# The order of a kernel's first transfers, on two queues in place of one, and half of its constant products

## The chip, the cores and the metric

One Trainium2 chip, one NeuronCore of it. The metric is device time in microseconds of one launch; the median of three runs of the kernel before is 424.43 us (423.6 to 425.7). Engines: PE is TensorE (matmul), PEld its weight load, DVE VectorE, ACT ScalarE, POOL GpSimd; SP is SyncE, which here only issues DMAs.

## The reference

2048 rows of 128 numbers pass through a feed-forward block, an attention block and the same feed-forward block again:

```python
x = x + 0.5 * ffn(layernorm(x), ...)   # the change is in this first one
x = x + attn(layernorm(x), ...)
x = x + 0.5 * ffn(layernorm(x), ...)

def ffn(x):                            # L=128 rows, N=16, D=128
    y1 = ln(x + mha(x))
    return ln(y1 + moe(y1))
def moe(x):                            # 8 experts, FF=512, at most S/8 rows each
    gates = softmax(x @ wg); idx = argmax(gates)
    # row kept if its place among the rows of its expert is under the cap
    h = disp @ w1 + b1;  y = h @ w2 + b2
    return where(keep, gate * y, 0)
```

The batch that `mha` attends over has one row, so its softmax is 1 and it is the product with the value weights and the output weights. No activation stands between `w1` and `w2`, so the two are multiplied to one 128x128 matrix per expert, and the biases to one row per expert.

## The kernel before

The 2048 rows are four chunks (g = 0 to 3) of four tiles of 128 rows. Each engine runs its own list of instructions. In the first feed-forward block the order on each engine is written by hand in the strings of ORDER; a word is a step and a chunk (or, for D and E, an expert or a tile). The engines meet only through semaphores.

The steps that matter here, all in the first block:

- X (DVE, POOL): statistics of the input rows of a chunk, waiting for its x_in, and the rsqrt on POOL.
- A (PE, ACT): transposes of the chunk (L1105) and the copy out. W (PE, DVE): the product of value and output weights, which waits for all six transfers of mha_in (L1169, L1172, L1175), with short runs of constant products between.
- P (PE, DVE, POOL): the product with that matrix (L1089), the addition on DVE (L780), statistics, and on POOL the rsqrt (L501). M (ACT): the normalised rows. C (PE, ACT): their transposes.
- D (PE): for expert e, waits for its two weights (w_in), then eight matmuls for w1 x w2 (L1199) and eight for its bias row (L1206). In D0, ahead of L1206, PE waits for b1_ready to be 2.
- b (POOL, L583): the copy that raises b1_ready to 2. It waits for fold_in to be 48, so for all three of b1_t, b2_t and sel.
- L, R, K: logits, the pick of the expert, its coefficient (the picks are L806 and L808 on DVE). B on POOL (L509): the addition of a bias to the input rows. H: the end of the folding. E: the experts of a tile.

The orders around the change, and the wait in step b:

```python
"pe":   "A0 W0 A1 P0 P1 D0 C0 D1 D2 L0 A2 C1 P2 R0 A3 D3 P3 K0 D4 L1 D5 D6 D7 R1 H0 K1 ..."
"act":  "A0 A1 M0 M1 C0 L0 A2 C1 A3 D0 K0 ..."
"dve":  "10 X0 X1 W0 X2 P0 P1 X3 L0 R0 P2 K0 P3 L1 ..."
"pool": "X0 X1 X2 b0 P0 P1 X3 D0 B0 B1 B2 B3 P2 P3 ..."

pool.wait_ge(fold_in, 16 * FOLD)          # FOLD = 3
pool.tensor_copy(b1_diag, b1_t).then_inc(b1_ready, 1)
```

Beside its work PE multiplies a constant tile by itself (keep_busy, L1157): START_WORK times at the start, and by IDLE_WORK before some steps, 12 times before C0 of the first block. Results of these are not read.

All loads are issued by SP: chunk 0 of x, the six of mha_in, chunks 1 to 3, the four of route_in, the three of fold_in, the four of const_in, then w1 and w2 of experts 0 to 7 (16 transfers of 256 KB), then what attention needs. ACT issues none.

Of the kernel before, what the change touches and what calls it, by code (L numbers as in the profile page):

```python
# [14 lines left out]
P = 128  # L15
# [3 lines left out]
G = 4  # L19
GT = T // G  # L20
GW = GT * P
E = 8
FF = 512
FC = FF // P
# [117 lines left out]
)  # L142


START_WORK = 20
IDLE_WORK = {"C0": (12, 0), "O3": (0, 4), "A3": (0, 3), "C3": (0, 26), "L3": (0, 4), "R3": (0, 7),
             "K3": (0, 2), "B3": (0, 1)}

# [6 lines left out]
def build(nc, a, out):  # L155
    with ExitStack() as ctx:
        def sb(name, shape, dt=F32):
            return ctx.enter_context(nc.sbuf_tensor(name, shape, dt))

        def sem(name):  # L160
            return ctx.enter_context(nc.semaphore(name))
# [4 lines left out]
        ident = sb("ident", [P, P])  # L166
# [7 lines left out]
        centre = sb("centre", [P, D])  # L174
# [34 lines left out]
        def rows(k):  # L209
# [28 lines left out]
        w1T = fold[:, 0:4096].rearrange("p (e c d) -> p e c d", e=E, c=FC)  # L238
        w2 = fold[:, 4096:8192].rearrange("p (e c d) -> p e c d", e=E, c=FC)
# [8 lines left out]
        wv = fold[:, 13568:13696]  # L248
        woT = fold[:, 13696:13824]
        bv = fold[:, 13824:13825]  # L250
        bv_rep = fold[:, 13952:14080]
        ob_rep = fold[:, 14080:14208]
# [21 lines left out]
        w_in = [sem(f"w_in{e}") for e in range(E)]  # L274
        packed_in, row_in = ([sem(f"{n}{c}") for c in range(G)] for n in ("packed_in", "row_in"))
        wo_in = sem("wo_in")
        const_in, mha_in, route_in, fold_in, att_in, rope_in, template_in = (sem(n) for n in
            ("const_in", "mha_in", "route_in", "fold_in", "att_in", "rope_in", "template_in"))
# [36 lines left out]
        def cols(g):  # L315
            return slice(GW * g, GW * (g + 1))
# [8 lines left out]
        def group(g):  # L325
            return slice(GT * g, GT * (g + 1))
# [9 lines left out]
        def normed_groups(kind):  # L336


            return {ROWS: 0, LN2: G - 1}.get(kind, G)
# [24 lines left out]
        def _(sp):  # L364
            def load_x(g):
                sp.dma_start(x_tm[:, group(g), :],
                             a["x"][cols(g), :].rearrange("(t p) d -> p t d", p=P)).then_inc(x_in[g], 16)

            load_x(0)
            for dst, src in ((ident[:], a["ident"]), (centre[:], a["centre"]), (wv, a["wv"]), (woT, a["woT"]), (bv, a["bv"]),  # L370
                             (ob_rep, a["ob"].partition_broadcast(P))):
                sp.dma_start(dst, src).then_inc(mha_in, 16)
            for g in range(1, G):
                load_x(g)
            for dst, src in ((g1c[:], a["g1c"]), (wg[:], a["wg"]), (tri_bf[:], a["tri"].bitcast(BF16)),
                             (rank[:], a["rank"].partition_broadcast(P))):
                sp.dma_start(dst, src).then_inc(route_in, 16)
            sp.dma_start(b1_t, a["b1_t"]).then_inc(fold_in, 16)
            sp.dma_start(b2_t, a["b2_t"]).then_inc(fold_in, 16)
            sp.dma_start(sel[:], a["sel"]).then_inc(fold_in, 16)  # L380
            for dst, src in ((lnb[:], a["lnb"].partition_broadcast(P)), (tile_is[:], a["tile_is"]),
                             (head_of[:], a["head_of"].bitcast(BF16)), (swap[:], a["swap"])):
                sp.dma_start(dst, src).then_inc(const_in, 16)
            for e in range(E):
                sp.dma_start(w1T[:, e, :, :], a["w1T"][e].rearrange("(p c) d -> p c d", c=FC)).then_inc(w_in[e], 16)
                sp.dma_start(w2[:, e, :, :], a["w2"][e].rearrange("(p c) d -> p c d", c=FC)).then_inc(w_in[e], 16)
            for dst, src in ((wqo[:, 0, :], a["wq"]), (wdu[:, 0, :], a["w_downT"]),
                             (wdu[:, 1, :], a["wk_up"]), (wdu[:, 2, :], a["wv_up"])):
                sp.dma_start(dst, src).then_inc(att_in, 16)
# [28 lines left out]
            for g in range(G):  # L418
                if g == HELD:
                    sp.wait_ge(branched, 1)  # L420
                for side in (1, 0):
                    w = 2 * g + 1 - side
                    sp.wait_ge(low_piece, w + 1)
                    dst = piece_dram[side, g].rearrange("b d two p n -> (d two p) b n")
# [27 lines left out]
            with sp.If(beyond_safe > 0):  # L452
# [11 lines left out]
                with sp.Fori(0, NG) as g:  # L464
# [4 lines left out]
                    dst = shift_dram[bass.ds(g * GH, GH), :].rearrange("h (t p) -> (h t) p", p=P)  # L469
# [156 lines left out]

        @block.scalar
        def _(act):
            def normalise(kind, n, g, src, dst):
                act.wait_ge(ln_offset[kind], normed_groups(kind) * n + g + 1)  # L630
                for t in range(GT * g, GT * (g + 1)):
                    ins = nc.scalar.activation(dst[:, t, :], src[:, t, :], ACT.Identity,  # L632
                                               bias=offset[:, t:t + 1], scale=rstd[:, t:t + 1])
                ins.then_inc(normed[kind], 1)
# [9 lines left out]
            def feed_forward(n):  # L644
                for step, g in steps(n, "act"):
                    q, bank = G * n + g, CHAIN + g % 2
                    if step == "A":
                        copy_turned(ROWS, n, g, bank, xT)
                    elif step == "M":
                        normalise(LN1, n, g, y, y)  # L650
                    elif step == "C":
                        act.wait_ge(route_in, 16 * ROUTE)
# [12 lines left out]
                    elif step == "E":  # L665
# [9 lines left out]
                        ins.then_inc(high_ready, 1)  # L675
                    elif step == "V":
                        normalise(LN2, n, g, y, y)
                    elif step == "S":
                        if g >= 2:
# [400 lines left out]
        def _(pe):  # L1080
# [73 lines left out]
            def keep_busy(count, bank=3):  # L1154

                for _ in range(count):
                    pe.matmul(ps[:, bank, :], idle[:, 0:P], idle[:], start=True, stop=True)  # L1157
# [131 lines left out]
            pe.wait_ge(idle_ready, 1)  # L1289
            keep_busy(START_WORK)  # L1290
            feed_forward(0)
# [12 lines left out]
            def scores(n, run):  # L1304

                k, _, banks = UNITS[n]
                c, g = BLOCKS[k]
                if n == 0 or UNITS[n - 1][0] != k and g == 0:
                    pe.wait_ge(packed_in[c], 16 * packed_dmas(c))
                    pe.wait_ge(row_in[c], 16 * SHIFT_DMAS)  # L1310
                if n < SLOTS:
                    slot_free(n)
                else:
                    pe.wait_ge(run.exp_done, n - SLOTS + 1)
                for i in range(len(banks[0])):
                    for b in range(2):
                        h, j, q, w, col = banks[b][i]
                        rows = slice(HALF * b, HALF * b + (USED if j >= GT * c else MASK_ROW))
                        pair = (GH * g + h) // 2
                        ins = pe.matmul(ps[:, 2 * (n % SLOTS) + b, col:col + w], tile_of(rows, 1, pair, j),  # L1320
                                        packed[rows, c, 0, pair, q - GW * c:q - GW * c + w], start=True, stop=True,
                                        tile_position=(HALF * b, 0))
                ins.then_inc(run.score_mm, 1)
# [185 lines left out]
```

## Time and profile before

| what | us |
|---|---|
| median of three runs | 424.43 |
| the profiled execution | 424.33 |
| its span | 422.5 |
| PE busy | 388.2 (92%) |
| ACT busy | 326.2 (77%) |
| DVE busy | 193.7 (46%) |
| POOL busy | 129.3 (31%) |

The span is the profiled execution from its first to its last recorded instruction; 1.8 us lie around it. Busy shares are of the whole span; a stage has its own. All times of rows below are counted from the start of the span. "Matmul busy" includes the constant products.

### The profile page before, as it was taken

Reading aid. Unit: us, or ns where it says so; the run is one execution under the profiler, and the core shown is the slowest. Engines: PE = TensorE matmul, PEld = TensorE weight load, DVE = VectorE, ACT = ScalarE, POOL = GpSimd, SP = SyncE. Lnnn points to the kernel's source line nnn. Section 1 sums busy time; section 2 is a strip of 40 time slices with the busy share of each in tenths; the row PEclk is TensorE's granted clock in tenths of the full one; section 3 lists DMA queues with packets and bytes.
Section 4 is the critical chain, followed back from the end, with each engine's and each line's share of the span. In section 5 each row is a group of like instructions: output and inputs, shape, how many; then the busy total and the mean of one; then the engine's idle time right before and its main releaser. Section 6 shows DMA issues by size and latency. Waiting matters only on the chain.

```text
span 422.5 us, 7542 instructions
## 1 busy us (share of the span) xinstructions
PE 388.2 (92%) x2708; PEld 130.5 (31%) x2711; DVE 193.7 (46%) x729; ACT 326.2 (77%) x466; POOL 129.3 (31%) x203
## 2 busy tenths in 40 slices
PE   7889999689979699999999999999999999999991
PEld 3577443234422132222222222222222222114530
DVE  4865698899844223314242232261332322303846
ACT  1245458386699689999999999999999999995131
POOL 1472788663210022100302210063122420110673
PEclk9999999999989799999999999999999999999996
DMA  5891900001993299600000000001000000000000
GB/s 143 294 347 26 116 2 2 0 1 63 237 256 52 87 217 252 98 2 2 0 2 2 0 2 2 0 2 28 0 2 0 2 27 0 2 2 0 1 26 25
DMA packets 17756, 24.52 MB, mean 58 GB/s; under 512 B 2616, under 2 KB 14584, under 8 KB 16632
## 3 DMA queue, kind: packets, MB, share of 16 engines
q1 hardware_dynamic: 17428, 23.91, 23.1%
q8 instruction: 23, 0.38, 0.4%
q0 software_dynamic: 288, 0.10, 0.2%
q14 instruction: 17, 0.14, 0.1%
HBM read 16.60 MB, written 7.41 MB: 57 GB/s over the span
## 4 chain that ended last, share of the span: by engine, by line
PE 55%; ACT 15%; DVE 11%; issue 10%; POOL 4%; DMA 1%; SPq 1%; ACTq 0%; DVEq 0%; POOLq 0%
PE ps L1342 22%; ACT arena L722 12%; PE ps L1320 12%; PE ps L1151 8%; PE ps L1089 2%; DVE arena L839 2%; DVE stats L749 2%; PE ps L1105 2%; PE ps L1199 1%; PE ps L1125 1%; PE ps L1147 1%; DMA x_tm<-in_x 1%; POOL arena L520 1%; PE ps L1271 1%; PE ps L1272 1%
## 5 line engine op out<-in xcount | busy, mean ns | idle before, releaser
L722 ACT ACTIVATE arena<-ps 128x1024 f32<-128x1024 f32 x272 | 253.5, 1068 | 12.2 <-PE ps L1320 11.3
L1342 PE MATMUL ps<-arena,v_st 128*9 128x512 f32 (+3 forms) x1280 | 146.6, 540 | 0.1
L1320 PE MATMUL ps<-packed 51*128 51x512 bf16 (+4 forms) x640 | 94.6, 355 | 9.4 <-issue 3.5
L501 POOL TENSOR_TENSOR rstd<-var_eps,neg_half 128x4 f32<-128x4 f32 x28 | 28.5, 1017 | 149.8 <-DVE var_eps L757 149.8
L1320 PEld LDWEIGHTS ps<-packed 51*128 51x128 bf16 (+1 forms) x640 | 23.6, 94 | 113.9 <-ACT arena L722 98.3
L520 POOL TENSOR_TENSOR arena<-trio 128x256 f32<-128x256 f32 x14 | 10.2, 726 | 88.3 <-DVE trio L839 88.3
L1342 PEld LDWEIGHTS ps<-arena,v_st 128*9 128x9 f32 x1280 | 20.7, 89 | 53.4 <-issue 38.2
L1151 PE MATMUL ps<-w,arena 128*128 128x512 f32 x64 | 31.0, 611 | 4.1 <-DVE arena L839 4.0
L839 DVE SCALAR_TENSOR_TENSOR trio<-ps,arena,trio 128x128 f32<-128x128 f32 x64 | 18.0, 344 | 34.1 <-PE ps L1151 32.5
L1151 PE MATMUL ps<-w,trio 128*128 128x512 f32 x64 | 33.5, 628 | 0.0
L984 DVE STREAM_TRANSPOSE o_t<-ps 128x512 f32<-128x512 f32 x16 | 11.5, 717 | 40.3 <-PE ps L1342 40.3
L673 ACT ACTIVATE arena<-ps,arena 128x128 f32<-128x128 f32 x64 | 17.9, 368 | 12.8 <-PE ps L1151 7.6
L1157 PE MATMUL ps<-idle 128*128 128x512 bf16 x82 | 21.4, 404 | 2.8 <-DVE idle L968 2.5
L1036 DVE TENSOR_SCALAR trio<-ps,arena 128x128 f32<-128x128 f32 x40 | 11.3, 345 | 26.1 <-PE ps L1151 26.1
L839 DVE SCALAR_TENSOR_TENSOR arena<-ps,arena 128x128 f32<-128x128 f32 x64 | 17.5, 341 | 3.5 <-ACT arena L673 1.9
L632 ACT ACTIVATE arena<-arena,offset,rstd 128x128 f32<-128x128 f32 x28 | 11.5, 484 | 9.7 <-POOL offset L504 9.7
L638 ACT ACTIVATE trio<-ps 128x512 f32<-128x512 f32 x9 | 5.4, 596 | 16.6 <-PE ps L1105 14.9
L1151 PEld LDWEIGHTS ps<-w,trio 128*128 128x128 f32 x64 | 10.3, 188 | 22.6 <-issue 22.6
L1151 PEld LDWEIGHTS ps<-w,arena 128*128 128x128 f32 x64 | 10.9, 189 | 20.1 <-issue 10.3
L545 POOL TENSOR_TENSOR arena<-arena,g_rep 128x512 f32<-128x512 f32 x8 | 10.1, 1272 | 21.7 <-PE ps L1105 21.7
L525 POOL TENSOR_TENSOR arena<-arena 128x128 f32<-128x128 f32 x32 | 15.6, 488 | 3.4 <-DVE arena L846 1.1
L529 POOL TENSOR_TENSOR arena<-arena 128x128 f32<-128x128 f32 x32 | 14.9, 465 | 2.5
(146 smaller groups left out, 405.2 us busy)
## 6 DMA issues: line engine op xcount, KB each, us to landing
packed<-piece_dram SPq DMA_DIRECT2D x16, 384.0 KB, 6.9
piece_dram<-packed SPq DMA_DIRECT2D x18, 256.0 KB, 3.6
packed<-in_w1T SPq DMA_DIRECT2D x8, 256.0 KB, 5.0
packed<-in_w SPq DMA_DIRECT2D x8, 256.0 KB, 5.4
trio<-in_rope SPq DMA_DIRECT2D x2, 1024.0 KB, 6.6
piece_dram<-trio SPq DMA_DIRECT2D x6, 256.0 KB, 9.5
packed<-in_template SPq DMA_DIRECT2D x2, 720.0 KB, 12.6
x_tm<-in_x SPq DMA_DIRECT2D x4, 256.0 KB, 5.4
```

The source lines that it names most:

```text
L501: pool.tensor_tensor(rstd[:, t], var_eps[:, t], neg_half[:], ALU.pow).then_inc(ln_rstd[kind], 1)
L520: pool.tensor_tensor(q, pair[n][:, t % 2, 0:2 * D], pair[n][:, t % 2, 2 * D:4 * D], ALU.add).then_inc(quad_ready, 1)
L525: pool.tensor_tensor(q[:, 0:D], q[:, 0:D], q[:, D:2 * D], ALU.add).then_inc(quad_ready, 1)
L529: pool.tensor_tensor(y[:, t, :], q[:, 0:D], base[:, t % (2 * GT), :], ALU.add).then_inc(z_ready, 1)
L632: ins = nc.scalar.activation(dst[:, t, :], src[:, t, :], ACT.Identity, bias=offset[:, t:t + 1], scale=rstd[:, t:t + 1])
L673: ins = nc.scalar.activation(prod[n][:, t % 2, cut], ps[:, t % 2, cut], ACT.Copy, scale=coef[n][:, t, e:e + 1])
L722: nc.scalar.activation(pexp[:, n % PB, :], ps[:, at:at + 2, :].rearrange("p b n -> p (b n)"), ACT.Exp, scale=SCALE).then_inc(run.exp_done, 1)
L839: ins = dve.scalar_tensor_tensor(pair[n][:, t % 2, D * e:D * (e + 1)], ps[:, bank, D * e:D * (e + 1)], coef[n][:, t, e:e + 1], prod[n][:, ...
L1151: pe.matmul(ps[:, bank, :], y1T[n][:, P * t:P * (t + 1)], w12[:, 512 * high:512 * (high + 1)], start=True, stop=True).then_inc(high_mm if ...
L1157: pe.matmul(ps[:, bank, :], idle[:, 0:P], idle[:], start=True, stop=True)
L1320: ins = pe.matmul(ps[:, 2 * (n % SLOTS) + b, col:col + w], tile_of(rows, 1, pair, j), packed[rows, c, 0, pair, q - GW * c:q - GW * c + w], ...
L1342: ins = pe.matmul(ps[32 * h:32 * h + VW, 6 + k % OB, q - GW * c:q - GW * c + w], v_st[:, j, GH * g + h, :], pexp[:, n % PB, 512 * b + col: ...
```

## The change

START_WORK is 10 in place of 20. SP issues all four chunks of x first, then route_in, b1_t, the weights of experts 1 to 7, and behind these b2_t and sel (the other two of fold_in) and const_in. ACT issues the six of mha_in, centre last, and the weights of expert 0, ahead of its first activation. Nothing else is changed: no wait, no order of steps, no size.

```diff
-START_WORK = 20
+START_WORK = 10
...
-            load_x(0)
-            for dst, src in ((ident[:], a["ident"]), (centre[:], a["centre"]), (wv, a["wv"]), (woT, a["woT"]), (bv, a["bv"]),
-                             (ob_rep, a["ob"].partition_broadcast(P))):
-                sp.dma_start(dst, src).then_inc(mha_in, 16)
-            for g in range(1, G):
+            for g in range(G):
                 load_x(g)
             for dst, src in ((g1c[:], a["g1c"]), (wg[:], a["wg"]), (tri_bf[:], a["tri"].bitcast(BF16)),
                              (rank[:], a["rank"].partition_broadcast(P))):
                 sp.dma_start(dst, src).then_inc(route_in, 16)
             sp.dma_start(b1_t, a["b1_t"]).then_inc(fold_in, 16)
+            for e in range(1, E):
+                sp.dma_start(w1T[:, e, :, :], a["w1T"][e].rearrange("(p c) d -> p c d", c=FC)).then_inc(w_in[e], 16)
+                sp.dma_start(w2[:, e, :, :], a["w2"][e].rearrange("(p c) d -> p c d", c=FC)).then_inc(w_in[e], 16)
             sp.dma_start(b2_t, a["b2_t"]).then_inc(fold_in, 16)
             sp.dma_start(sel[:], a["sel"]).then_inc(fold_in, 16)
             for dst, src in ((lnb[:], a["lnb"].partition_broadcast(P)), (tile_is[:], a["tile_is"]),
                              (head_of[:], a["head_of"].bitcast(BF16)), (swap[:], a["swap"])):
                 sp.dma_start(dst, src).then_inc(const_in, 16)
-            for e in range(E):
-                sp.dma_start(w1T[:, e, :, :], a["w1T"][e].rearrange("(p c) d -> p c d", c=FC)).then_inc(w_in[e], 16)
-                sp.dma_start(w2[:, e, :, :], a["w2"][e].rearrange("(p c) d -> p c d", c=FC)).then_inc(w_in[e], 16)
...
         @block.scalar
         def _(act):
+            for dst, src in ((ident[:], a["ident"]), (wv, a["wv"]), (woT, a["woT"]), (bv, a["bv"]),
+                             (ob_rep, a["ob"].partition_broadcast(P)), (centre[:], a["centre"])):
+                act.dma_start(dst, src).then_inc(mha_in, 16)
+            act.dma_start(w1T[:, 0, :, :], a["w1T"][0].rearrange("(p c) d -> p c d", c=FC)).then_inc(w_in[0], 16)
+            act.dma_start(w2[:, 0, :, :], a["w2"][0].rearrange("(p c) d -> p c d", c=FC)).then_inc(w_in[0], 16)
```

## Rows read from the trace of the kernel before

**Rows 1.** The chain of waits, 0 to 45 us: start, length, what it ran through.

```profile
4.14 5.22 DMA x_tm<-in_x
...
11.12 0.50 PE ps L1172 x2
...
17.18 1.02 POOL rstd L501
...
18.50 1.66 ACT arena L632 x4
...
20.20 0.66 PE ps L1105 x4
...
23.55 1.01 PE ps L1125 x8
...
28.19 1.05 DVE arena L780 x4
...
31.29 0.27 PE ps L1142
```

**Rows 2.** Timeline of SP's queue: start, us, line, transfer issued.

```profile
0.73 0.44 SPq L366 DMA_DIRECT2D x_tm<-in_x  x1
...
3.67 0.43 SPq L372 DMA_DIRECT2D packed<-in_ob  x1
4.14 1.54 SPq L366 DMA_DIRECT2D x_tm<-in_x  x3
...
8.94 0.43 SPq L379 DMA_DIRECT2D packed<-in_b_t  x1
9.41 0.43 SPq L380 DMA_DIRECT2D sel<-in_sel  x1
...
11.71 0.43 SPq L385 DMA_DIRECT2D packed<-in_w1T  x1
...
19.55 0.45 SPq L389 DMA_DIRECT2D wqo<-in_wq  x1
```

**Rows 3.** DMA view, 0 to 60 us: KB each, us from issue to landing.

```profile
packed<-in_ob SPq DMA_DIRECT2D x1, 64.0 KB, 4.8
...
wqo<-in_wq SPq DMA_DIRECT2D x1, 64.0 KB, 5.9
...
sel<-in_sel SPq DMA_DIRECT2D x1, 16.5 KB, 2.8
```

**Rows 4.** Timeline of all engines, 0 to 14 us: the constant products.

```profile
2.53 6.21 PE L1157 MATMUL ps<-idle 128*128 128x512 bf16 x20 [2.53 <-DVE idle L968]
...
4.21 0.15 PEld L1157 LDWEIGHTS ps<-idle 128*128 128x128 bf16 x1 [0.28 <-issue]
...
4.64 0.15 PEld L1157 LDWEIGHTS ps<-idle 128*128 128x128 bf16 x1 [0.28 <-issue]
```

**Rows 5.** The same view, 13.5 to 42 us: D0, C0 and the additions on GpSimd.

```profile
15.52 0.24 POOL L583 COPY packed<-packed 128x32 f32<-128x32 f32 x1
...
16.46 0.43 PE L1206 MATMUL ps<-packed 128*32 128x128 f32 x8
...
17.05 2.54 PE L1157 MATMUL ps<-idle 128*128 128x512 bf16 x11 [0.16 <-issue]
...
23.20 4.94 POOL L509 TENSOR_TENSOR arena<-x_tm,lnb 128x512 f32<-128x512 f32 x4
```

**Rows 6.** The same stretch: a product of step P2, the picks of two chunks.

```profile
25.89 1.13 PE L1089 MATMUL ps<-w_mha,trio 128*128 128x128 f32 x8 [0.42 <-ACT trio L638]
...
26.89 1.30 DVE L808 TENSOR_TENSOR pick<-arena,row_pick 128x32 f32<-128x32 f32 x1
...
35.35 0.18 DVE L808 TENSOR_TENSOR pick<-arena,row_pick 128x32 f32<-128x32 f32 x1
```

**Rows 7.** Stretches: length, busy us (instructions) of PE, PEld, DVE, ACT, POOL; granted clock; DMA share; GB/s.

```profile
139.10:142.58 3.48, 0.86 (x10) 0.13 (x10) 2.15 (x5) 2.23 (x3) 0.00 (x0) 1.00 0.02 5
142.58:146.00 3.42, 2.54 (x12) 0.29 (x12) 0.00 (x0) 1.89 (x2) 0.00 (x0) 0.50 0.33 110
```

## The prediction, made before the changed kernel ran

> **What bounds the kernel now.** I read the page's busy shares first, then the chain of waits, then the timeline of the first 45 us, because every transfer that moves is issued there. Over the span PE is the bound, but not in the first 31 us. In the chain of waits [rows 1] the first 20 us are latencies: chunk 1 of x holds DVE until 9.36 (4.14 + 5.22); W follows it on DVE and PE (11.12); then the rsqrt of P0 on POOL (17.18), the normalisation on ACT (18.50) and the transposes C0 at 20.20. From C0 the chain is PE (D1, D2, logits at 23.55), then DVE (28.19), then K0 on PE at 31.29. From there PE works almost without a gap to beyond 41 us (D4, L1, D5 to D7, R1, H0), and the experts wait for it. So the end of the kernel moves by what K0 moves, and K0 hangs on C0.
>
> **The first loads.** SP hands out about one transfer per 0.5 us. Now x has 0.73, then comes mha_in to 4.1, and x's other chunks between 4.14 and 5.68 [rows 2]. After the change the four chunks are out by 0.73 + 4 x 0.51 = 2.8, and ACT hands out mha_in from about 0.7 to 3.5, so both land earlier: ob, issued at 3.67, took 4.8 us and closed mha_in at 8.5 [rows 2, 3]; with its issue at about 2.6 and centre's at 3.1 I estimate 6 to 7. ACT has nothing else to do then. PE's twenty constant products end at 8.74 (2.53 + 6.21) [rows 4]; two of them start 0.43 us apart at the low clock, the later ones run twice as fast, so ten fewer are 10 x 0.215 = 2.2 us and A0 can start at 6.6. W's second product, at 11.12 now, could come at 6.6 + 0.6 (transposes) + 0.1 + 1.0 (four constant products) = 8.3. The front is 2.8 us ahead, if nothing else is late.
>
> **What is late next: fold_in.** Step b on POOL waits for b1_t, b2_t and sel. Two of them now come behind the weights of experts 1 to 7. Behind b on POOL stand the rsqrts of P0, P1 and X3 and the additions B; on PE the second half of D0 waits for b, and behind it stand the twelve constant products, C0 and all the rest. Call F the time at which fold_in is complete; before it is 9.41 + 2.8 = 12.2 [rows 2, 3] and no one waited for it long (b at 15.52 came behind X2).
>
> F after the change: route_in and b1_t take SP from 5.68 to 8.94 now, 3.26 us [rows 2], so the first weight goes out at 2.8 + 3.2 = 6.0. From the first weight's issue (11.71) to the landing of wq (19.55 + 5.9 = 25.45), the small transfer right behind all 16 weights, 13.7 us pass [rows 2, 3]. Its 5.9 us against sel's 2.8 show that a small transfer queues behind the weights ahead of it. Take off the 2.8 and an eighth of the other 10.9 for the pair that is gone: 12.4 us for seven pairs. With an idle queue F = 6.0 + 12.4 = 18.4. But x, mha_in, expert 0 and route_in (1.05 + 0.32 + 0.52 + 0.13 = 2.0 MB by their sizes) are in the way. At the weights' rate (4.19 MB in 10.9 us, 0.38 MB/us) they take 5.3 us from about 1.8 and are gone at 7.1, just when the first weight would start: nothing to add. At the rate of x now (chunks 1 to 3 and ob, 0.85 MB in about 4 us, 0.21) x and mha_in take 6.6 and the rest 1.7: gone at 10.1, 3.0 to add, F = 21.4. I take 0.6, near the first, since the slow stretch now is one behind ob's broadcast. F = 19.0. From below F is bounded by SP alone: 14 issues of 0.49 (7.84/16 between 11.71 and 19.55) put b2_t at 12.9 and sel at 13.4, and 2.8 more make 16.2.
>
> The Trainium skill, page "DMA: Bandwidth & Descriptors", section "Issuing engines are not separate DMA queues", says that DMAs of all issuing engines run on the same 16 DMA engines and interleave, so that a second issuer saves issue time alone. No row here has a DMA of ACT's. By this rule ACT's 0.84 MB are in x's and the weights' way, as counted; without it they would not be, and F would be 18.4 flat.
>
> **From F to C0.** b takes 0.24 and a hop 0.06, D0's second half 0.43 [rows 5]: PE is at its constant products at F + 0.75 = 19.75. P1 on PE would be done near 12 and D0's first half near 13.3, so PE has been idle for some 6 us. At 139 us PE was busy in 0.86 of 3.48 us, and in the stretch that followed 0.50 of the clock was granted, which is 1.2 of 2.4 GHz [rows 7]. So I expect 1.2 GHz at 19.75. At the start, 6.21 us for 20 products means about 9 at 0.43 and 11 at 0.215 [rows 4]; so here 9 x 0.43 + 3 x 0.215 = 4.5 us in place of 2.54 [rows 5]. C0 = 19.75 + 4.5 = 24.25, against 20.20: 4.05 late. The other way to C0 is earlier: P0 on POOL at F + 0.3, and 20.20 - 17.18 = 3.0 on to C0 [rows 1] is 22.3. START_WORK and the earlier x are worth nothing in this sum: their 2.8 us lie under the wait for F.
>
> **From C0 to K0.** D1, D2 and L0 follow as before, 4.05 late. Then something comes back. Before, POOL's additions (23.20 to 28.14) lay beside the picks on DVE: the pick at 26.89 took 1.30 us, the same instruction at 35.35, with POOL free, 0.18 [rows 5, 6]. After, POOL begins the additions at 19.3 + 3 rsqrts of 1.02, two offsets of 0.2, D0's 0.9 and gaps of 0.3 = 23.9 and ends at 28.9, before the picks at about 30. So DVE waits no longer for its picks but for the product P2 on PE, which ended at 27.02 before [rows 6], while the addition began only at 28.19 [rows 1]. 1.15 comes back, and K0 is 4.05 - 1.15 = 2.9 late. The dense stretch of PE carries 2.9 to the end.
>
> **The sum.** The profiled execution took 424.33 (span 422.5 and 1.8 around it), 0.1 under the median. 424.33 + 2.9 = 427.2, or 427.3 against the median of 424.43. The forecast's own range: F = 21.4 adds 2.4 more, 429.7; F = 17.5, adding half of the issue bound's distance, takes off 1.5, 425.8.
>
> **Rivals.** About 0.5%, 2.1 us, is what a measurement of this kernel can tell from no change.
>
> 1. *sel does not queue behind the weights* (ends on the other side). Then F = 13.4 + 2.8 = 16.2. D0 ends at 16.95, and with the clock kept up (PE idle for 3 us alone) the twelve products take 2.54: C0 at 19.5, by POOL and ACT too (16.5 + 3.0). 0.7 early, and the picks still meet POOL's additions: 424.43 - 0.7 = 423.7. It decides for a faster kernel from F under 16.9. For it: b2_t and sel are small. Against: wq, as small, took 5.9 us. The Trainium skill, same page, section "Queues, rings and completion order", says that completion is not first in, first out per issuing engine, as a later transfer may finish its write first; by it sel could come out ahead, though its descriptors are taken in ring order. 0.17.
> 2. *The clock stays at 2.4 GHz over PE's wait*, or comes back at once. C0 = 19.75 + 2.54 = 22.3, 2.1 late; the picks at 28.2 still meet the end of the additions, some 0.7 comes back: 1.4 late, 425.8. Against it are rows 7, for it only that the two gaps are not alike. 0.17.
> 3. *The change does what it says*: F is under cover (under 13.5) and the whole 2.8 arrives, 421.6. For this SP would have to hand out its 14 weights in half the time. 0.06.
> 4. Inside all cases: where later gaps of PE fall against the clock's drops. Before, 142.58 to 146.00 ran at 0.50 [rows 7]; one such stretch of 3.4 us more or less costs or gives up to 1.7 us. It is in the range and shifts no centre.
>
> **How the numbers follow.** The forecast has 0.60. The range: below it reaches rival 1, 423.7, and leaves out rival 3; above, 429.5. Slower by over 0.5% (above 426.55) is most of the forecast's case, less its early F, and a little of rival 2 with an unlucky clock: 0.58. Faster by over 0.5% (below 422.3) is rival 3 and the lucky end of rival 1: 0.08. Within 0.5%: 0.34.
>
> **What would show it.** In the profile after: SP's first weight issued near 6; fold_in's last landing near 19; POOL's L583 at 19 in place of 15.52, with a wait ahead for DMA; PE idle for some 6 us ahead of D0's L1206, then constant products 0.43 apart; C0 near 24.2; the picks at 0.2 us each; K0 near 34.2. Chunk 1 should land near 5.5 and W be done by 10, to no avail. Wrong would be: L583 before 17 (the queue), constant products at 0.215 throughout (the clock), or K0 late by as much as C0 (the picks).

## The result, and the profile after

The changed kernel takes 433.86 us (median of 4 runs, 433.25 to 433.99) against 425.06 for the kernel before: ratio 1.0199 (1.0159 to 1.0238), so 2% slower. The profiled execution took 433.92, its span is 432.0 (424.33 and 422.5 before): 8.8 us more between medians, 9.6 between the two profiled executions. Two runs of about 717 us, one of the kernel before and one of experiment 1, and the longest run of experiment 8 stand outside the ratios. The forecast had the sign and the place, and a third of the size: 427.3, range to 429.5.

The chain of waits after (start, length, what it ran through):

```profile
4.39 2.33 SPq L373
...
15.29 8.47 DMA sel<-in_sel
...
23.89 0.24 POOL packed L579
...
24.18 0.65 PE ps L1208 x8
...
25.17 4.62 PE ps L1159 x11
29.79 0.44 PE ps L1107 x4
...
36.42 1.14 DVE arena L782 x4
...
39.61 0.27 PE ps L1144
```

From 4.39 to 15.25 the chain is SP's queue; then sel's transfer, 8.47 us, holds it until 23.76. Only then comes POOL's copy of step b (before: 15.52 [rows 5]), D0's second half at 24.18 (16.46), the twelve constant products in 4.62 us in place of 2.54 (of the twelve, eleven are recorded in both traces), and the transposes C0, whose first instruction starts at 29.63 by the timeline (20.20 [rows 1]). K0 is at 39.61 in place of 31.29.

```profile
29.63 0.60 PE L1107 MATMUL ps<-ident,arena 128*128 128x128 f32 x4
```

SP's queue, and from the DMA view the us from issue to landing:

```profile
0.73 2.10 SPq L366 DMA_DIRECT2D x_tm<-in_x  x4
...
4.39 2.33 SPq L373 DMA_DIRECT2D rank<-in_rank  x1
...
7.41 0.43 SPq L376 DMA_DIRECT2D packed<-in_w1T  x1
...
15.29 0.44 SPq L379 DMA_DIRECT2D sel<-in_sel  x1
```

```profile
packed<-in_ob ACTq DMA_DIRECT2D x1, 64.0 KB, 5.8
centre<-in_centre ACTq DMA_DIRECT2D x1, 64.0 KB, 7.2
...
rank<-in_rank SPq DMA_DIRECT2D x1, 64.0 KB, 8.7
...
sel<-in_sel SPq DMA_DIRECT2D x1, 16.5 KB, 8.5
```

The first weight goes out at 7.41 (11.71 before [rows 2]), sel at 15.29. sel takes 8.5 us to land where it took 2.8 [rows 3]. And mha_in did not come early: centre, issued by ACT at 3.11, took 7.2 us and closed it at 10.3, against 8.5 before.

The front of the timeline, five stretches after and one before (start:end, length, busy us of PE, PEld, DVE, ACT, POOL with counts, granted clock, DMA share, GB/s):

```profile
3.11 0.45 ACTq L627 DMA_DIRECT2D centre<-in_centre  x1
...
10.30 0.23 DVE L865 COPY packed<-packed 128x128 f32<-128x128 f32 x1 [2.99 <-DMA centre<-in_centre]
...
10.41 1.09 PE L1107 MATMUL ps<-ident,x_tm 128*128 128x128 f32 x4 [4.11 <-DMA centre<-in_centre]
...
13.43 0.63 PE L1174 MATMUL ps<-packed 128*128 128x128 f32 x2
```

```profile
1.80:6.30 4.50, 3.77 (x10) 1.21 (x10) 3.04 (x16) 1.28 (x1) 0.30 (x1) 1.00 0.85 230
6.30:10.40 4.10, 0.00 (x1) 0.02 (x1) 1.04 (x9) 0.00 (x0) 1.72 (x2) 0.82 0.78 215
18.90:24.10 5.20, 0.00 (x0) 0.00 (x0) 4.81 (x32) 0.00 (x0) 0.21 (x2) 0.85 0.85 243
24.10:29.80 5.70, 5.29 (x21) 2.16 (x23) 0.00 (x0) 3.18 (x8) 5.46 (x9) 0.54 0.90 364
91.40:98.20 6.80, 6.57 (x8) 2.33 (x9) 5.82 (x14) 3.19 (x8) 6.18 (x11) 0.54 0.00 1
```

```profile
6.30:10.40 4.10, 4.06 (x22) 1.89 (x20) 0.98 (x6) 0.60 (x1) 0.09 (x1) 1.00 0.92 216
```

DVE and PE wait for mha_in until 10.3. W's second product comes at 13.43, not at 8.3 as forecast and not at 11.12 as before. From 6.3 to 10.4 the DMA engines moved 215 GB/s at 0.78 of their time; with one queue they moved 216 in the same stretch (the second fence, 0.92 of their time), so in it the second queue brought no rate. From 18.9 to 24.1 PE does nothing, waiting for fold_in; from there to C0 the granted clock is 0.54, the lower of its two levels for most of the stretch.

One more difference lies at 91 us, where the queries and keys are projected; two pairs of products of PE, and the first pair before:

```profile
91.26 2.05 PE L1265 MATMUL ps<-trio,wkv 128*128 128x512 f32 x2
93.53 2.05 PE L1265 MATMUL ps<-trio,wq 128*128 128x512 f32 x2 [0.23 <-DVE arena L841]
```

```profile
82.93 1.10 PE L1263 MATMUL ps<-trio,wkv 128*128 128x512 f32 x2 [0.22 <-ACT arena L673]
```

The first pair took 1.10 before and started at 82.93, so it is 8.33 late, as K0 is. Here it runs at half clock (0.54 in the row of 91.40:98.20), in a stretch that ran at 1.00 before (82.9 to 89.9). The end of the span is 9.5 late: 1.2 us were lost there, and on balance nothing after it.

### The profile page after: what moved, and what is told of

Same layout as the page of the kernel before. It is cut to its first block, busy times and chain, and to the rows that moved or that the text cites. A ratio compares the mean times of both kernels' runs of the same rounds, so it can differ in the third digit from the quotient of the medians.

```text
span 432.0 us, 7522 instructions
## 1 busy us (share of the span) xinstructions
PE 392.4 (91%) x2698; PEld 132.9 (31%) x2701; DVE 192.1 (44%) x729; ACT 325.9 (75%) x466; POOL 128.7 (30%) x203
## 3 DMA queue, kind: packets, MB, share of 16 engines
q1 hardware_dynamic: 16276, 23.06, 21.4%
HBM read 16.60 MB, written 7.41 MB: 56 GB/s over the span
## 4 chain that ended last, share of the span: by engine, by line
PE 55%; ACT 15%; issue 10%; DVE 9%; SPq 4%; POOL 3%; DMA 3%; ACTq 0%; DVEq 0%; POOLq 0%
PE ps L1344 21%; ACT arena L724 12%; PE ps L1322 12%; PE ps L1153 9%; PE ps L1091 2%; DMA sel<-in_sel 2%; DVE arena L841 2%; PE ps L1127 2%; PE ps L1107 1%; PE ps L1201 1%; PE ps L1159 1%; DVE stats L751 1%; PE ps L1149 1%; DMA piece_dram<-packed 1%; DVE arena L919 1%
## 5 line engine op out<-in xcount | busy, mean ns | idle before, releaser
L1159 PE MATMUL ps<-idle 128*128 128x512 bf16 x72 | 22.4, 458 | 3.0 <-DVE idle L970 2.5
L1153 PEld LDWEIGHTS ps<-w,trio 128*128 128x128 f32 x64 | 10.3, 188 | 22.6 <-issue 22.6
L1153 PEld LDWEIGHTS ps<-w,arena 128*128 128x128 f32 x64 | 10.9, 189 | 20.1 <-issue 10.3
```

What stands on the lines that cost most here:

```text
L1153: pe.matmul(ps[:, bank, :], y1T[n][:, P * t:P * (t + 1)], w12[:, 512 * high:512 * (high + 1)], start=True, stop=True).then_inc(high_mm if ...
```

## The experiments

Comparisons were made in four groups. The kernel before ran in each; its median there was 424.68, 424.25, 425.23 and 425.24. C0 and K0 below are from one profile of each kernel, so each also carries that run's own clock. Theories A to H are named in the expectations (theory F is not the time F of the prediction).

**1. fold_in ahead of the weights, else as changed.**

```diff
             sp.dma_start(b1_t, a["b1_t"]).then_inc(fold_in, 16)
+            sp.dma_start(b2_t, a["b2_t"]).then_inc(fold_in, 16)
+            sp.dma_start(sel[:], a["sel"]).then_inc(fold_in, 16)
             for e in range(1, E):
...
-            sp.dma_start(b2_t, a["b2_t"]).then_inc(fold_in, 16)
-            sp.dma_start(sel[:], a["sel"]).then_inc(fold_in, 16)
```

> The changed kernel with b2_t and sel issued right behind b1_t, ahead of the weights. Theory A (POOL's and TensorE's wait for fold_in is the loss, and the late mha_in only a lesser part): step b no longer waits, its place is right behind X2 near 18.4; C0 then follows the rsqrt of P0 (statistics done at 19.9 in the changed kernel) by 3.0, near 22.9 in place of 29.8 and of 20.2 before, so the kernel takes 425.1 + 2.7 = about 427.8, less up to 1 for the picks. Rival B (the two queues and the ten missing products cost it, by a late mha_in and the low clock): it stays within 1.5 us of 433.9.

Measured: 427.42 us, ratio 1.0062 (1.0032 to 1.0092). Step b and C0 in its timeline:

```profile
16.97 0.24 POOL L579 COPY packed<-packed 128x32 f32<-128x32 f32 x1
```

```profile
21.65 0.66 PE L1107 MATMUL ps<-ident,arena 128*128 128x128 f32 x4 [1.14 <-ACT arena L634]
```

Of the 8.8 us that the change cost over the kernel before, 2.7 are left (427.42 - 424.68) after moving two small transfers.

**2. One queue and twenty products as before, b2_t, sel and const_in behind all weights.**

```diff
+            for e in range(E):
+                sp.dma_start(w1T[:, e, :, :], ...).then_inc(w_in[e], 16)
+                sp.dma_start(w2[:, e, :, :], ...).then_inc(w_in[e], 16)
             sp.dma_start(b2_t, a["b2_t"]).then_inc(fold_in, 16)
             sp.dma_start(sel[:], a["sel"]).then_inc(fold_in, 16)
...
-            for e in range(E):
-                sp.dma_start(w1T[:, e, :, :], ...).then_inc(w_in[e], 16)
-                sp.dma_start(w2[:, e, :, :], ...).then_inc(w_in[e], 16)
```

> The kernel before, one queue and twenty products, with b2_t, sel and const_in moved behind all sixteen weights. Theory A: first weight issued near 8.9, fold_in complete near 22.7, TensorE idle for some 7 us ahead of D0's second half, its twelve constant products at the low clock, C0 near 28 and the kernel at 431 to 433. Rival B: within 1.5 us of the kernel before, 425.1.

Measured: 433.58 us, ratio 1.0207 (1.0137 to 1.0277). In its timeline:

```profile
24.30 0.23 POOL L583 COPY packed<-packed 128x32 f32<-128x32 f32 x1 [8.80 <-DMA sel<-in_sel]
...
25.57 4.72 PE L1157 MATMUL ps<-idle 128*128 128x512 bf16 x11 [0.33 <-issue]
...
30.13 0.60 PE L1105 MATMUL ps<-ident,arena 128*128 128x128 f32 x4
```

With its own front undisturbed this kernel loses all that the change loses (8.9 us), and the products at 4.72 us and C0 at 30.13 are as in the changed kernel. Together with 1 this shows the cause from both sides. It does not follow that the rest costs nothing: here sel sits behind eight pairs, not seven.

**3. The kernel before with ten products.**

> The kernel before with ten constant products at the start, nothing else. Theory A: mha_in lands at 8.5, TensorE waits 2.1 us for it from 6.4, W's second product waits for chunk 1 as before: 425.1, within 1 us. Rival C (the ten products held the clock): it falls near 9.5, W, A1 and P0 run at 1.2 GHz and C0 is 1 to 2 us late, 426 to 427.

Measured: 425.30 us, ratio 1.0015 (0.9983 to 1.0048). PE's first instructions:

```profile
2.53 4.45 PE L1157 MATMUL ps<-idle 128*128 128x512 bf16 x10 [2.53 <-DVE idle L968]
8.41 1.09 PE L1105 MATMUL ps<-ident,x_tm 128*128 128x128 f32 x4 [1.43 <-DMA packed<-in_ob]
...
9.71 1.85 PE L1157 MATMUL ps<-idle 128*128 128x512 bf16 x4
11.40 0.39 PE L1172 MATMUL ps<-packed 128*128 128x128 f32 x2
```

After the wait for mha_in the four transposes take 1.09 and the four constant products 1.85 us, the low clock (0.63 and 1.03 before), but W's second product comes at 11.40 against 11.12, since before it waited for DVE, which had chunk 1 to do. C0 is at 20.37, 0.2 late. The 1 to 2 us of rival C don't show in the median, though the interval reaches to 0.5%.

**4. As 1, with twenty products.**

> The first of these with twenty constant products again. TensorE would be busy to 8.7 and then wait 1.6 us for mha_in (10.3 in the changed kernel). Theory A with C: the clock stays up, W and P0 come 1.9 us earlier than with ten, and the kernel takes 1.5 to 2 us less than the first, about 426. Without C: the same time as the first.

Measured: 426.74 us, ratio 1.0053 (1.0011 to 1.0094). C0 is at 19.97 in its profile, 1.7 us before that of 1, and K0 at 31.55, 1.4 before, but the median is only 0.7 less, inside the two intervals. The gain at C0 is seen in one profile; in the time it isn't shown.

**5 and 6. What held the DMA engines.** In 5 bv is loaded as 128 rows of 512 bytes; in 6 ob and rank are read from full copies instead of 128 times from one row.

```diff
-(bv, a["bv"])                              # 5
+(bv_rows, a["bv"])                         # [128, 128] in memory, bv is column 0
-(ob_rep, a["ob"].partition_broadcast(P))   # 6
+(ob_rep, a["ob"])                          # [128, 128] in memory
-(rank[:], a["rank"].partition_broadcast(P))
+(rank[:], a["rank"].rearrange("p (t e) -> p t e", e=E))
```

> The changed kernel with bv loaded as 128 rows of 512 bytes (its value repeated) in place of 128 single numbers of 4 bytes. In the changed kernel fold_in was complete at 23.8 and mha_in at 10.3, and the DMA rate fell to 138 GB/s near 6 us, when bv was under way. Theory D (tiny packets hold up their queue): mha_in complete 1 us or more earlier, fold_in about 1 us earlier, kernel about 432.5. Rival E (the rate is held by the broadcasts ob and rank): both stay within 0.4 us, kernel within 1 us of 433.9.

> The changed kernel with ob and rank read from full copies of 128 rows in memory in place of 128 reads of one row of 512 bytes each. Rival E: rank's issue on SP takes 0.5 us in place of 2.33, the first weight goes out near 6.0 in place of 7.4, fold_in is complete 2 us or more earlier, near 21.5, kernel near 431.5. Theory D: at most 0.5 us earlier.

Measured, one run each: 433.04 us for 5 and 428.75 for 6. Of 6, SP's queue, the landings, and the stretch 6.3 to 10.4:

```profile
4.48 0.43 SPq L373 DMA_DIRECT2D rank<-in_rank  x1
...
5.45 0.49 SPq L376 DMA_DIRECT2D packed<-in_w1T  x1
...
12.93 0.43 SPq L379 DMA_DIRECT2D sel<-in_sel  x1
```

```profile
packed<-in_ob ACTq DMA_DIRECT2D x1, 64.0 KB, 4.8
centre<-in_centre ACTq DMA_DIRECT2D x1, 64.0 KB, 5.0
...
rank<-in_rank SPq DMA_DIRECT2D x1, 64.0 KB, 5.7
...
sel<-in_sel SPq DMA_DIRECT2D x1, 16.5 KB, 7.6
```

```profile
6.30:10.40 4.10, 2.78 (x16) 1.50 (x14) 1.34 (x10) 0.60 (x1) 1.77 (x2) 1.00 1.07 337
```

centre lands 2.2 us sooner after its issue, rank 3.0 sooner, the same stretch moves 337 GB/s in place of 215. SP hands out rank in 0.43 us where it took 2.33, and the first weight at 5.45 (forecast for the change: 6.0; measured 7.41). W's second product is at 9.85, step b at 20.65, C0 at 25.50, 4.1 earlier than in the changed kernel, K0 at 35.48, also 4.1. The run is 5.2 shorter: beyond the 4.1, the pairs of products at the projections take 1.10 here, not 2.05. This bears out rival E for landings and rate. Theory D is half seen: in 5 step b came at 22.30, 1.6 earlier, and the run is 0.9 shorter, but centre landed 7.0 after its issue (7.2), and step b alone differs by 0.5 between two kernels that are the same up to there (23.89, and 23.43 in experiment 9). One run of each, against a spread of 3 us or so between runs, shows the sign and the order of size, no more; how much of 5 is D stays open.

**7. Both, with fold_in ahead and twenty products.**

> Two queues, fold_in ahead of the weights, twenty constant products, bv in rows and ob and rank as full copies: what the change could be. If D or E holds, mha_in is complete by 8 and W's second product, 11.0 in the kernel with fold_in ahead, comes at 9.5, C0 near 18.6 against 20.2 before: the kernel at 425.1 - 1.5 = 423.6. If neither, as the kernel with fold_in ahead, 426.7.

Measured: 426.27 us, ratio 1.0027 (0.9990 to 1.0063). A miss: W's second product came at 11.16 and C0 at 20.13. Centre landed at 8.3; the twenty products weren't done: A0 started at 9.64 behind them.

**8. ACT issues mha_in alone; all weights on SP, behind fold_in; twenty products.**

> Two queues with mha_in alone on ACT, all eight pairs of weights on SP behind fold_in, twenty constant products. Theory F (expert 0's 512 KB on ACT's queue take DMA time from x and route_in): the later chunks and fold_in land about 1.3 us earlier (0.52 MB at 0.38 MB/us), but expert 0's weights land later, near 12; C0 near 20 as before, kernel within 1.5 us of 425.1. Without F: nothing lands earlier.

Measured: 426.89 us (422.42 to 429.51), ratio 1.0048 (1.0018 to 1.0078). Rank's issue and landing:

```profile
4.45 0.43 SPq L373 DMA_DIRECT2D rank<-in_rank  x1
```

```profile
rank<-in_rank SPq DMA_DIRECT2D x1, 64.0 KB, 5.9
```

Its profile is of its shortest run, C0 at 18.89, granted clock 0.986 over the span; the other nine had 0.964 to 0.983. Theory F holds for the landings: centre 5.0 us after its issue against 6.2 in experiment 4, rank 5.9 against 7.2, A0 at 8.39 against 9.46. So expert 0's weights on ACT's queue were a second part of what delayed the changed kernel's front, and not one that adds up with the first: centre lands 5.0 after its issue without the broadcasts (6), without these weights (here) and without both (11). SP's hold at rank too is gone here (0.43), with both broadcasts in place; it took the two together. In the time nothing of it is seen: these ten runs are no faster than those of 4. Why both stay 0.5% behind the kernel before, with C0 not late in either profile, isn't shown.

**9. As changed, without the twelve products ahead of C0.**

```diff
-IDLE_WORK = {"C0": (12, 0), ...
+IDLE_WORK = {"C0": (0, 0), ...
```

> The changed kernel without the twelve constant products ahead of C0, which took 4.6 us at the low clock behind the late D0. Theory G (they stand on the path for nothing here): C0 follows ACT's rows, ready near 27.2, 2.4 us earlier than 29.6, and the kernel takes 433.9 - 2.4 = 431.5. Theory H (they buy the clock for D1, D2 and L0): C0 is 2.4 us earlier, but the next 3 to 4 us of TensorE run at 1.2 GHz and take it back: 433 to 434.

Measured: 430.65 us, ratio 1.0122 (1.0060 to 1.0185), 3.2 below the changed kernel. TensorE from step b on:

```profile
23.75 0.65 PE L1208 MATMUL ps<-packed 128*32 128x128 f32 x8 [5.25 <-POOL packed L579]
26.64 1.12 PE L1107 MATMUL ps<-ident,arena 128*128 128x128 f32 x4 [2.24 <-ACT arena L634]
27.55 1.92 PE L1201 MATMUL ps<-packed 128*128 128x128 f32 x8
29.40 0.66 PE L1208 MATMUL ps<-packed 128*32 128x128 f32 x8
```

C0 waits for ACT's rows alone and comes 3.0 earlier, of which 0.5 is the earlier step b of this run. As H has it, C0's transposes and D1 run at half clock (1.12 and 1.92 where 0.60 and 1.06 stood), and at K0, 38.55, 1.1 of the 3.0 is left. But the median is 3.2 lower, more than G claimed. In the profiled run, 1.0 of the advance is there at the projections (90.22 against 91.26) and the span ends 2.1 earlier (429.9):

```profile
90.22 1.10 PE L1265 MATMUL ps<-trio,wkv 128*128 128x512 f32 x2 [0.22 <-ACT arena L675]
```

This pair takes 1.10 in place of 2.05: the stretch at half clock that costs the changed kernel 1.2 is missing. That accounts for the rest in these two profiles; for the other runs it isn't shown.

**10. The kernel before with full copies of ob and rank.**

> The kernel before with ob and rank read from full copies, nothing else. If 128 reads of one row hold up the single queue too, mha_in is complete near 7 in place of 8.5 and chunk 1 near 8.4 in place of 9.4, W and C0 come about 1 us earlier, and the kernel takes 424.5 - 1 = 423.5. If the queue is held by SP's issue, nothing moves: within 0.5 us of 424.5.

Measured: 424.37 us, ratio 0.9978 (0.9948 to 1.0008). In the profile ob lands 2.3 us after its issue (4.8 before [rows 3]), W's second product is at 9.91 and C0 at 18.88, 1.3 earlier. K0 is at 29.98, 1.3 earlier too, but the span ends only 0.5 earlier (422.0). The time is 0.9 less in the median, and the interval reaches a little past 1.

**11 and 12. As 8, with full copies; twenty products and ten.**

> Two queues with mha_in alone on ACT, fold_in ahead of all weights, twenty constant products, ob and rank as full copies. The version with broadcasts had W's second product at 9.9 and C0 at 18.9 in its profile. With copies TensorE's twenty products end at 8.7 and bind W, so at most 0.5 us more: C0 near 18.5, 1.7 ahead of before. The front's gain carried to the end would give 423; but that version's median was 2 us over the kernel before in spite of 1.3 us ahead at C0, by a lower clock later. If that is chance of where TensorE's gaps fall, this one lies between 422.5 and 426; if it comes with an earlier front, near 426.5.

> Two queues with mha_in alone on ACT, fold_in ahead of all weights, ob and rank as full copies, and ten constant products in place of twenty. With twenty, the products ended at 9.54 in one profile and at 8.39 in another, depending on when the clock rose, and A0 stood behind them, while mha_in was complete near 8.1. With ten they end near 6.4 and A0 starts at 8.1: W's second product near 9.6 and C0 near 18.6, 1.5 us ahead of the version with twenty in its profile, if the clock stays up over 1.7 us of waiting. Then 425.0 - 0.7 to 1.5, about 424, against 424.6 before. If the clock does not stay up, as the version with fold_in ahead and ten products against twenty: 0.7 later, 425.7.

Measured: 11 takes 425.00 us, ratio 1.0006 (0.9975 to 1.0038); 12 takes 424.78, ratio 0.9977 (0.9954 to 0.9999). PE at the start of 11, then A0, C0 and a step of POOL in 12:

```profile
2.53 7.17 PE L1157 MATMUL ps<-idle 128*128 128x512 bf16 x20 [2.53 <-DVE idle L968]
9.54 0.60 PE L1105 MATMUL ps<-ident,x_tm 128*128 128x128 f32 x4
```

```profile
8.33 0.63 PE L1105 MATMUL ps<-ident,x_tm 128*128 128x128 f32 x4 [1.50 <-DMA centre<-in_centre]
```

```profile
18.85 0.66 PE L1105 MATMUL ps<-ident,arena 128*128 128x128 f32 x4 [1.13 <-ACT arena L632]
...
21.58 0.87 POOL L572 TENSOR_SCALAR lnb<-lnb 128x256 f32<-128x256 f32 x1 [0.66 <-DMA swap<-in_swap]
```

In 11 the products took 7.17 us (6.21 before [rows 4]) and A0 stood behind them, though centre had landed at about 8.1. With ten, A0 is at 8.33 and C0 at 18.85. But K0 is at 30.61, only 0.7 earlier than before, where 10 with the same C0 has 29.98: const_in lies behind the weights here, POOL waits 0.66 us for its last transfer, swap, and so its additions and the picks beside them come later. The same wait is there in 4 (0.46) and 8 (1.66). Version 12 has the lowest ratio of all, 0.2% under the kernel before by an interval that ends at 0.9999, no better than 10, which has one queue.

## Why the prediction was wrong, step by step

**The place was right.** Step b waits for fold_in, PE stands behind it, C0 and K0 follow (experiments 1 and 2). Rival 1, that sel overtakes the weights, is refuted: it took 8.5 us. Rival 3 is too.

**The term that was mis-sized is F**: forecast 19.0, measured 23.76, 4.8 late and outside my upper bound of 21.4. The step that failed is the choice of 0.6 us for the traffic ahead of the weights, "since the slow stretch now is one behind ob's broadcast". I saw that the broadcast was slow, and took its move to another queue for a cure. It wasn't one: from 1.8 to 6.3 us the engines moved 230 GB/s and from 6.3 to 10.4 215, the rate of my upper bound (0.21 MB/us) and not the 0.38 near which I chose. At these rates the 2.0 MB are gone near 10.8; by the prediction's own sum, which counted the weights' start at 7.1, that adds 3.7 in place of 0.6 and gives 22.1 (an estimate). The last 1.7 us stay open. The late first weight (7.41, not 6.0) is no loss of its own: in experiment 9 it went out at 8.33, and sel, issued at 15.98, landed at 23.3 all the same.

Experiment 6 takes the broadcasts away and step b comes 3.2 us earlier. That is most of the miss, by one run. Expert 0's weights on ACT's queue delay the front by about 1 us (4 against 8); what they alone do to F wasn't tried. But even in 6 sel lands at 20.5 (12.93 + 7.6), with the first weight out at 5.45: the 0.6 was too little without them too.

The sentence on the Trainium skill, page "DMA: Bandwidth & Descriptors", section "Issuing engines are not separate DMA queues", stands, and the traces agree: with expert 0's weights on ACT's queue SP's rank took 7.2 us to land, without them 5.9 (4 and 8). I had counted ACT's bytes, at the wrong rate.

**The front** was forecast 2.8 ahead and was 2.3 late (13.43 against 11.12). mha_in came at 10.3, not "6 to 7", for the same reason; PE waited 4.1 us for it, and the granted clock fell meanwhile (0.82 over 6.3 to 10.4). It lay under F's wait, so it cost nothing in the changed kernel; in experiment 1, where F is gone, it is what remains.

**From F to C0**: 29.63 - 23.76 = 5.9, forecast 5.25. The clock was low as in the rows at 142.58 us [rows 7] (0.54 from 24.1 to 29.8); rival 2 is refuted. The twelve products took 4.62 (forecast 4.5); of the other 0.5, D0's second half is 0.2 (0.65 us, 0.43 before).

**From C0 to K0**: C0 9.4 late, K0 8.3: 1.1 came back, forecast 1.15, and for the reason given: POOL's additions ended at 33.4, the pick at 35.46 took 0.19 us, and the addition at 36.42 waited for PE.

**To the end**: K0's 8.3 reach 91 us whole, then 1.2 are added by a stretch at low clock that was not there before: rival 4, which I had put at up to 1.7 and left out of the centre. The sum: 2.9 (forecast) + 4.8 (F) + 0.6 (F to C0) + 1.2 = 9.5, the growth of the span.

## What to carry to other kernels

A semaphore that counts several transfers is complete with the last; before moving transfers, list for each semaphore which member is now last and what engine waits for it first. A small transfer late in a queue costs what lies ahead of it: 2.8 us became 8.5. And what a second issuing queue brings must be worked out from DMA time, not from issue time: from 6.3 to 10.4 us two queues moved 215 GB/s where one had moved 216, and ob, slow in one queue (4.8 us), was slow in two (5.8).

## What the runs showed that I had not expected

- Reading one row of 512 bytes 128 times is dear: 4.8 us to land where full copies took 2.3 (experiment 10). In the changed kernel SP was held 2.33 us at issuing rank; without the broadcasts (6) or without expert 0's weights on ACT's queue (8) it was 0.43.
- The time of one kernel's runs goes with the mean granted clock. Over 83 runs of the kernel before, the 16 with a mean granted clock above 0.980 took 423.5 us in the mean, the 29 at 0.975 or less took 426.5. So an advance of 1.3 us at C0, plain in a profile, needs ten or more runs to show in the median, and in experiment 8 didn't.
- One place after K0 takes or gives more than the front did. The second pair of products at the projections takes 2.04 or 2.05 us in the profiles of the changed kernel and of 1 to 5, 7 and 12, and 1.10 in those of the kernel before and of 6, 8 and 9. In 3, K0 is 0.2 late and the span 1.8 longer. These are single profiles, and why the clock is low there in one and not in the other isn't shown.
